# Attention heads, start of each pass: first branch's norm split in two, query split released earlier, weight split moved, nine unread products removed

## The reference

```python
q, k1, v1 = ...                       # k1, v1 through a latent of 32
o1 = softmax(q k1^T / 8 + causal) v1                 # branch 0: all earlier tokens
o2 = softmax(q ks^T / 8) vs                          # branch 1: 256 selected tokens
o3 = softmax(q kw^T / 8 + window of 64) vw           # branch 2: the last 64 tokens
o  = g[0] * o1 + g[1] * o2 + g[2] * o3               # gates of the batch
t  = t + o @ Wproj
```

## Time and profile before

| | |
|---|---|
| time, median of 3 runs | 2594.59 us (2593.18 to 2597.10) |
| the profiled execution's own time | 2595.74 us |
| its span, first to last instruction | 2593.5 us |
| busy: PE, PEld | 2346.2 us (90%), 1701.4 us (66%) |
| busy: DVE, ACT, POOL | 1814.3 us (70%), 1410.9 us (54%), 1261.7 us (49%) |
| mean granted clock of TensorE | 0.954 |

### The profile page before, as it was taken

How to read it: one execution, slowest core, us unless ns; L and a number is a source line. 1 busy time by engine, 2 the same in 40 slices (tenths; PEclk the granted TensorE clock), 3 DMA queues, 4 the chain that set the end, 5 groups by cost and what they waited for, 6 DMA issues and landing times. The chain is left out here.

```text
span 2593.5 us, 51536 instructions
## 1 busy us (share of the span) xinstructions
PE 2346.2 (90%) x16829; PEld 1701.4 (66%) x16829; DVE 1814.3 (70%) x3640; ACT 1410.9 (54%) x2487; POOL 1261.7 (49%) x966
## 2 busy tenths in 40 slices
PE   6889978766999999999999999999999999999866
PEld 4666655554676767767676676766766776675655
DVE  5868757875768677686777768677686767766536
ACT  2135544433576665666666575665666656575223
POOL 1106671001374664846557375664746657373245
PEclk8999998878999999999999999999999999999778
DMA  3040300112411112111220212112111220210233
GB/s 121 1 104 10 90 11 16 63 38 57 142 38 41 41 39 55 24 47 37 46 59 16 55 37 45 44 32 55 30 41 37 46 58 16 55 21 17 79 116 101
DMA packets 82188, 128.13 MB, mean 49 GB/s; under 512 B 15824, under 2 KB 58240, under 8 KB 81728
## 3 DMA queue, kind: packets, MB, share of 16 engines
q1 hardware_dynamic: 77616, 119.47, 18.4%
q0 software_dynamic: 3024, 7.43, 0.9%
q10 hardware_dynamic: 1472, 0.24, 0.1%
HBM read 61.26 MB, written 20.79 MB: 32 GB/s over the span
## 5 line engine op out<-in xcount | busy, mean ns | idle before, releaser
L2671 ACT ACTIVATE a_PT<-PS 128x512 f32<-128x512 f32 (+1 forms) x1104 | 584.2, 565 | 365.3 <-PE PS L2527 244.1
L2381 POOL TENSOR_TENSOR a_KT<-a_PT 128x256 f32<-128x256 f32 (+2 forms) x175 | 349.5, 2008 | 457.9 <-ACT a_PT L2671 449.4
L2740 DVE TENSOR_REDUCE a_NM<-PS 128x2 fp32r<-128x512 f32 (+2 forms) x512 | 290.8, 612 | 131.8 <-PE PS L2471 72.7
L2381 POOL TENSOR_TENSOR a_KT<-a_KT,a_PT 128x1024 f32<-128x1024 f32 (+1 forms) x122 | 370.9, 3040 | 8.5
L2521 PE MATMUL PS<-a_QH,a_K 128*128 128x512 f32 (+3 forms) x768 | 292.0, 390 | 1.1 <-ACT a_PT L2671 1.0
L2752 DVE TENSOR_REDUCE a_MX<-PS 128x1 f32<-128x512 f32 (+3 forms) x432 | 265.9, 665 | 32.5 <-PE PS L2486 18.0
L2521 PE MATMUL PS<-a_QH,a_KSW 128*128 128x192 f32 (+3 forms) x832 | 264.6, 339 | 12.1 <-DVE a_NM L2740 10.5
L2486 PE MATMUL PS<-a_K,a_QH 128*128 128x512 f32 (+3 forms) x768 | 252.4, 404 | 9.3 <-DVE a_K L2727 7.9
L2522 PE MATMUL PS<-a_QL,a_K1B 76*128 76x512 f32 (+3 forms) x768 | 259.4, 348 | 0.0
L2471 PE MATMUL PS<-a_KSW,a_QH 128*128 128x256 f32 (+2 forms) x1024 | 196.8, 304 | 4.1 <-DVE a_QL L2724 4.1
L2471 PEld LDWEIGHTS PS<-a_KSW,a_QH 128*128 128x128 f32 x1024 | 162.4, 192 | 49.2 <-DVE a_NM L2740 19.4
(11 more groups left out here) (436 smaller groups left out, 5193.7 us busy)
## 6 DMA issues: line engine op xcount, KB each, us to landing
a_KWB<-a_KSW SPq DMA_DIRECT2D x64, 256.0 KB, 3.3
a_K1B<-a_K SPq DMA_DIRECT2D x32, 512.0 KB, 4.8
a_XC<-latents SPq DMA_DIRECT2D x16, 512.0 KB, 3.8
a_CKS<-latents SPq DMA_DIRECT2D x16, 512.0 KB, 4.6
a_CF<-latents SPq DMA_DIRECT2D x16, 448.0 KB, 4.1
slots<-in_empty_slots SPq DMA_DIRECT2D x1, 5160.0 KB, 19.8
f_XB<-slots SPq DMA_DIRECT2D x8, 645.0 KB, 5.7
c_EX<-in_experts SPq DMA_DIRECT2D x1, 4608.0 KB, 17.9
```

What stands on the lines that cost most here:

```text
L2381: nc.gpsimd.tensor_tensor(total, one_in, other_in, ALU.add).then_inc(s["added"], 1)
L2671: nc.scalar.activation(PT[:, to:to + width], turning(key)[:, 0:width], ACT.Exp).then_inc(s["taken"], 1)
L2740: nc.vector.tensor_reduce(NM[:, i, DH:].rearrange("p (h x) -> p h x", x=3)[:, h:h + 2, x], ring(key)[:, 0:2 * w].rearrange("p (h n) -> p h ...
```

## The change

Four edits, all at the begin of a pass or in what it issues:

1. `norm.z` keeps the first transpose alone; reciprocal, second transpose and multiplication become a step of their own, `scale.z` (`weigh_sums`). For z = 1 to 5 it stands right behind `norm.z`, so nothing moves. For z = 0 `norm.0` stays at the end of the pass ahead and `scale.0` stands behind `near.7.3`. Every wait for a finished norm becomes one for `scale`.
2. For the queries' groups ACT writes rows 0 to 63 from PSUM, signals a new semaphore `upper`, waits for it itself, and writes rows 64 to 127 as a copy of rows 0 to 63 of `QH`, from SBUF. DVE's split waits for `upper`, no longer for all four. `near_scores` waits for both the split and the copies.
3. `wk` moves from the begin of the table to behind `v.v1.1`.
4. `keep_clock(9, bank)` is gone.

```diff
 ORDER = """
-wk tr.q2 tr.q3 split.tr.q2 split.tr.q3
+tr.q2 tr.q3 split.tr.q2 split.tr.q3
...
-score.5.3 near.5.1 near.5.2 v.v1.1 near.5.3 near.6.0 value.4.4 near.6.1 near.6.2 near.6.3 turn.0.2 near.7.0 value.5.5 add.7 near.7.1 near.7.2 k1.0 near.7.3
-score.6.0 split.k1.0 k1.1 sum.1 norm.1 turn.0.3 k1.2 split.k1.1 split.k1.2
+score.5.3 near.5.1 near.5.2 v.v1.1 wk near.5.3 near.6.0 value.4.4 near.6.1 near.6.2 near.6.3 turn.0.2 near.7.0 value.5.5 add.7 near.7.1 near.7.2 k1.0 near.7.3 scale.0
+score.6.0 split.k1.0 k1.1 sum.1 norm.1 scale.1 turn.0.3 k1.2 split.k1.1 split.k1.2
...
                     after(pe, q, at, bank_free(key, q))
-                    if i == 4 and n == 0:
-                        keep_clock(9, bank)
-                    after(pe, q, at, *(("reduced", ("split", "tr", g)) for g in made))
+                    after(pe, q, at, *(("reduced", ("split", "tr", g)) for g in made),
+                          *(("copied", ("tr", g)) for g in made if g[0] == "q"))
...
                     after(act, q, at, ("filled", key))
-                    for rows in (slice(0, DH), slice(DH, 128))[:2 if g[0] == "q" else 1]:
+                    high = {"q": QH, "w": KW, "s": KS}[g[0]]
+                    for e in range(2):
+                        last = nc.scalar.activation(odd_even(high, e, slice(0, DH), tokens(g)),
+                                                    ring(key)[e * DH:(e + 1) * DH, :].rearrange("p (u c) -> p u c", u=2),
+                                                    ACT.Copy, scale=0.125 if g[0] == "q" else 1.0)
+                    if g[0] == "q":
+                        last.then_inc(s["upper"], 1)
+                        after(act, q, at, ("upper", key))
                         for e in range(2):
-                            last = nc.scalar.activation(odd_even({"q": QH, "w": KW, "s": KS}[g[0]], e, rows, tokens(g)),
-                                                        ring(key)[e * DH:(e + 1) * DH, :].rearrange("p (u c) -> p u c", u=2),
-                                                        ACT.Copy, scale=0.125 if g[0] == "q" else 1.0)
+                            last = nc.scalar.activation(odd_even(high, e, slice(DH, 128), tokens(g)),
+                                                        odd_even(high, e, slice(0, DH), tokens(g)).bitcast(F32), ACT.Copy)
                     last.then_inc(s["copied"], 1)
...
                 def split(key, q, at):
-                    after(dve, q, at, ("copied", key))
+                    after(dve, q, at, ("upper" if key[0] == "tr" and key[1][0] == "q" else "copied", key))
...
+                def weigh_sums(z, q, at):
+                    p, bank = plan.half[z], P[6 + z % 2]
                     own = z < 4 and z % 2 == 0
-                    after(dve, q, at, summed, ("normal", ("norm", (z - 1) % ZS)))
-                    nc.vector.transpose(RT[:, :], sums).then_inc(s["by_query"], 1)
                     after(dve, q, at, ("by_query", ("norm", z)))
```

More of the change, by code:

```diff
@@ L2030 @@
 score.13.0
-score.13.1 far.6.4 far.6.5 join.5 sum.2 norm.2 +a.s
+score.13.1 far.6.4 far.6.5 join.5 sum.2 norm.2 scale.2 +a.s
 score.13.2
-score.13.3 +rot.s far.6.6 far.6.7 value.12.12 add.16 sum.3 norm.3 value.13.13 +a.w0 +rot.w0 join.6 far.7.0
+score.13.3 +rot.s far.6.6 far.6.7 value.12.12 add.16 sum.3 norm.3 scale.3 value.13.13 +a.w0 +rot.w0 join.6 far.7.0
 score.14.0 far.7.1
@@ L2047 @@
 score.18.2
-score.18.3 +v.vw.0 +rope.q0 +tr.q0 sum.4 +split.tr.w1 norm.4 value.17.17 value.18.18 add.21 +split.tr.q0 +a.w2 +rot.w2 +a.q1
+score.18.3 +v.vw.0 +rope.q0 +tr.q0 sum.4 +split.tr.w1 norm.4 scale.4 value.17.17 value.18.18 add.21 +split.tr.q0 +a.w2 +rot.w2 +a.q1
 score.19.0
@@ L2067 @@
 score.24.0 +near.3.2 +near.3.3 +a.w3 +a.q2 +rot.q2
-+score.0.0 +turn.0.1 value.22.22 add.25 value.23.23 value.24.24 add.26 +rot.w3 add.27 sum.5 norm.5
++score.0.0 +turn.0.1 value.22.22 add.25 value.23.23 value.24.24 add.26 +rot.w3 add.27 sum.5 norm.5 scale.5
 +score.0.1
@@ L2149, in count_events, with events @@
         found = {}
-        def events(name, *whats, times=1, credit=0):
+        def events(name, *whats, times=1, credit=0, only=None):
             rows = [(at, tuple(st[1:]), st[0]) for at, st in enumerate(self.steps) if st[1] in whats]
+            rows = [row for row in rows if only is None or only(row[1])]
             if name == "weighed":
@@ L2161, in count_events @@
         events("reduced", "near", "far", "split")
+        events("upper", "tr", only=lambda key: key[1][0] == "q")
         events("joined", "join")
@@ L2167, in count_events @@
         events("by_query", "norm", credit=8)
-        events("inverted", "norm")
-        events("by_row", "norm")
-        events("normal", "norm", credit=12)
+        events("inverted", "scale")
+        events("by_row", "scale")
+        events("normal", "scale", credit=12)
         events("y_added", "ysum", credit=8)
@@ L2384, in branch_sum @@
                     p = plan.half[z]
-                    after(pool, q, at, ("normal", ("norm", z)))
+                    after(pool, q, at, ("normal", ("scale", z)))
                     if z < 4:
@@ L2535, in values @@
                         made = [("copied", {0: ("v", "v1", 1), 1: ("v", "vs", 0), 2: ("v", "vw", 1)}[x]),
-                                ("residual", ("project", z + 4)) if z < 2 else ("normal", ("norm", z - 2))]
+                                ("residual", ("project", z + 4)) if z < 2 else ("normal", ("scale", z - 2))]
                     if by_product(z, q) and k0 == plan.first[z]:
@@ L2760, in normalise @@
                 def normalise(z, q, at):
-                    p, bank = plan.half[z], P[6 + z % 2]
                     sums, summed = turning(("sum", z)), ("scored", ("sum", z))
@@ L2764, in normalise @@
                         sums, summed = P[0], ("weighed", ("value", plan.final[z]))
+                    after(dve, q, at, summed, ("normal", ("scale", (z - 1) % ZS)))
+                    nc.vector.transpose(RT[:, :], sums).then_inc(s["by_query"], 1)
+                def weigh_sums(z, q, at):
+                    p, bank = plan.half[z], P[6 + z % 2]
                     own = z < 4 and z % 2 == 0
-                    after(dve, q, at, summed, ("normal", ("norm", (z - 1) % ZS)))
-                    nc.vector.transpose(RT[:, :], sums).then_inc(s["by_query"], 1)
                     after(dve, q, at, ("by_query", ("norm", z)))
                     nc.vector.reciprocal(RQ[:, :], RT[:, :].rearrange("p (b r) -> p b r", r=32)[:, :, 0]).then_inc(s["inverted"], 1)
-                    after(dve, q, at, ("inverted", ("norm", z)))
+                    after(dve, q, at, ("inverted", ("scale", z)))
                     nc.vector.transpose(RT[:, :].rearrange("p (b r) -> p b r", r=32),
                                         RQ[:, :, None].broadcast_to([128, HALF // 32, 32])).then_inc(s["by_row"], 1)
-                    after(dve, q, at, ("by_row", ("norm", z)), ("weighed", ("value", plan.final[z])),
+                    after(dve, q, at, ("by_row", ("scale", z)), ("weighed", ("value", plan.final[z])),
                           not own and ("y_added", ("ysum", {1: 5, 3: 1, 4: 3, 5: 4}[z])))
@@ L2802, in one_pass @@
                             normalise(key[1], q, at)
+                        elif what == "scale":
+                            weigh_sums(key[1], q, at)
                         elif what == "project":
```

## The result

The change takes 2677.32 us, median of 4 runs (2673.38 to 2678.25), against 2593.93 of the kernel before beside it: ratio 1.031, 95% interval [1.0296, 1.0324], slower by 83 us. The forecast had the direction, and 27 us; the time lies above its range.

What follows compares the result with a forecast made beforehand. The prediction took PE, 90% busy, as the bound. Head, `wk` and `scale.0` together cost 0.95 us a pass, 15 us; the clock added 12: 2594.59 + 27 = 2622 us, range 2602 to 2638.

Steps and rivals of the forecast that it cites:

- head, with products gone: Start of a pass, up to `score.4.3`: PE gains 0.3 us a pass (0 to 0.7), as ACT's first exponential holds it.
- scale.0 behind near.7.3: DVE's scaling before `split.k1.0` delays `norm.1` and stalls PE at `k1.2`: 0.75 us or so a pass lost.
- wk in the middle: DVE's weights' subtraction before `near.5.3` delays the banks of `near.6.2` and `near.6.3`: loss 0.5 us a pass (0 to 1.0).
- clock: Behind the idle at the head, PE's clock falls in eight more passes, ten in all, at 1.5 us each: 12 us.
- The wait for ACT: Before the weights' subtraction, DVE waits for ACT to round the weights behind `v.v1.1`'s copy: about 1 us.
- The price of 1.5 us: Each clock fall at the head costs 1.5 us, not 1.65, as part lies under the wait for ACT.
- The faster one: Rival: the head's 2.5 us come through, with ACT not the limit; 1.25 us a pass gained, 2575 us, chance 0.09.
- the head's 2.5 us: At the head, `near.4.0` starts 2.5 us earlier; the forecast let only 0.3 of it reach PE's later work.
- No difference: Rival: idle time and waits absorb the moved steps, each pass 0.3 us or less either way; 2590 to 2599 us, chance 0.08.
- no more falls: Rival: the clock at the head falls no oftener than now, leaving only the 15 us loss; 2610 us, chance 0.27.

Runs made afterwards that it cites:

- p3: The kernel before with only `wk` moved to behind `v.v1.1`; norm, split and unread products as before: 2667.57 us, ratio 1.029.
- e4: The change with POOL's addition for the second branch issued as two instructions of two heads each: 2636.65 us, one run.
- e2: The change with `wk` placed behind `near.7.0`, where POOL's addition is over: 2621.23 us, ratio 1.0083.
- e1: The change with `wk` back at the front of the table, the other three edits kept: 2617.86 us, ratio 1.010.
- p4: The kernel before with only the nine unread products removed: 2621.32 us, ratio 1.0104.
- b3: e1 with `scale.0` behind q2's split and q3's transposes, copies and split behind `near.4.3`, without the products: 2586.43 us, ratio 0.9963 to the kernel before.

## Why the prediction was wrong, step by step

The four terms, for 16 passes, against the account above (idle time by the view of waits, clock by what PE's busy time grew, the products left out):

| term | forecast, us | measured, us |
|---|---|---|
| head, with products gone | -5 | -11 (9.8 idle more, 21 of products less) |
| scale.0 behind near.7.3 | +12 | +7 |
| wk in the middle | +8 | +42 |
| clock | +12 | +44 |

The last row is busy time, and it holds more than the clock: by the lengths of passes the falls cost 31 us, and `wk`, 3.0 us a pass in p3, costs 48.

**The step that failed: wk in the middle.** "DVE waits for that, then subtracts for 0.41", and "No other queue is passed: SP and POOL issue nothing in these steps". The wait for ACT was right, 1.14 us measured against about 1. The duration was not: 3.05. I asked which instructions the step issues and which queues it passes, not what runs on POOL at the moment to which it goes. The row was there to be read: in the kernel before POOL's addition runs from 891.47 to 896.02, and the forecast itself had the subtraction begin at 893.2, inside it. A duration was carried over from a place where POOL was idle. The mechanism is shown by e4 (POOL's instruction cut in half, DVE's falls from 3.05 to 0.90) together with e2 (the same fresh operand, POOL idle, 0.42), and the price by p3, where nothing else was changed. The Trainium skill states it, "SBUF — State Buffer", section "Who interferes with whom": a VectorE instruction with two inputs from SBUF contends with a GpSimd instruction that reads SBUF, and the one that is issued first has the shared pair of ports for its whole instruction while the other stands still. The traces agree in each point: 3.05 with POOL at work, 0.38 to 0.42 without, the end 0.28 behind POOL's. By that rule the subtraction would have lasted from 893.2 to 896.02, and the term, if all of that reaches PE, is 16 x (896.02 - 893.2) = 45 us, an estimate from rows of before, against the 42 of idle time measured. That one operand in SBUF is not enough for it, the trace of before shows too. This instruction of the same operation, with its other operand in PSUM, lies inside such an addition and takes its usual 0.69:

```profile
953.52 0.69 DVE L2775 TENSOR_TENSOR a_YB<-PS,a_RT 128x512 f32<-128x512 f32 x1 [0.21 <-DVE a_RT L2771]
950.84 4.56 POOL L2381 TENSOR_TENSOR a_KT<-a_PT 128x2048 f32<-128x2048 f32 x1 [2.11 <-ACT a_PT L2671]
```

A small slip besides: the forecast's 893.93 is the second product of `near.6.1`; `near.6.2` went out at 894.04.

**The clock: right cause, wrong place and too small.** Forecast were eight more falls behind the head's wait, ten in all. In e1 and p4, where `wk` stands at the front and the products are gone, the clock falls at 13 and 14 heads, so that reasoning held and the count was low (between 2 and 16 the middle of the upper half, by which ten was taken, is 12 or 13). The price of 1.5 us held in e1, where a pass with a fall takes 112.41 us and one without 110.85. In p4 it didn't: 11 of the 14 falls show 0.50 for six us, not three, and such a pass takes 112.64 against 110.23. In the change itself the clock falls at the head in four passes only. In 13 it falls behind the 2.6 us of idle at `near.6.2`, which the forecast did not have. Why it lasts longer there than in most passes of p3, where the idle spot is the same, I have not settled; the two differ in the head, where the change has two waits and no products. The range's high end took 1.25 us a pass where the working had 1.5 for the loss in full; with 1.5 it would be 2642, still below the time measured.

**The head: right.** ACT held `score.4.3`: its first exponential began 4.81 us behind its first copy (before 4.85), and PE waited 1.64 for it. The gain was 0.59 and not 0.3, since the two lower copies took 1.15 us from SBUF where two from PSUM took 1.20: cheaper by a little, where I had added 0.2 for four. ACT's timeline of the change:

```profile
891.16 1.20 ACT L2630 ACTIVATE a_QH<-PS 64x512 fp32r<-64x512 f32 x2 [3.15 <-PE PS L2441]
892.40 1.15 ACT L2637 ACTIVATE a_QH<-a_QH 64x512 fp32r<-64x512 f32 x2
...
895.97 1.09 ACT L2678 ACTIVATE a_PT<-PS 128x512 f32<-128x512 f32 x2
```

**scale.0: right, a little dear.** No idle is left between the split and the norm of DVE (915.78 + 1.39 = 917.17, next at 917.21, against the 1.07 of the earlier trace rows):

```profile
915.78 1.39 DVE L2734 TENSOR_TENSOR a_K<-PS,a_K 64x512 fp32r<-64x512 f32 x2
917.21 0.72 DVE L2772 STREAM_TRANSPOSE a_RT<-PS 128x512 f32<-128x512 f32 x1
```

and `k1.2` waits 0.53 where 0.75 was taken.

**The rivals.** The faster one asked for a first exponential before 884.6; it came at the old distance, and the head's 2.5 us did not come through. "No difference" falls with the result, "no more falls" with the 13 passes of the change in which the clock fell.

## What to carry to other kernels

Before an instruction is moved, look up what the other engines do at its new place, GpSimd above all: the duration of a VectorE instruction with two SBUF operands holds only for a place where no long GpSimd instruction reads SBUF. Work that nobody reads can be worth more than it costs: here 21 us of it held back a clock loss, and it could go only where the wait ahead of it had been cut in two (b3). And a wait that is removed is worth what the next holder leaves (here ACT's queue of copies), so find that holder first and reorder it, as b3 does.

## What the runs showed of the hardware that was not expected

- VectorE's maxima, which read PSUM, are not held up by the same addition of GpSimd: two in 1.16 us beside it, one in 0.56 without it.
- The hold goes by instruction. Of two additions 0.08 us apart the subtraction waited out the first and ended 0.19 us into the second, which took 4.58 us; such an addition takes 4.57 in e2, where the subtraction comes behind its end.
- One wait of 1.7 us without dense work behind it brought the clock down at 14 of 15 heads (p4); two waits of 0.8 us, 6 us apart, brought it down at none (b3).
